# Two-layer cross attention on one core: another order of the calls on all five engines

## The reference

```python
x = L0(x, ctx_768)      # (64, 128, 320), context (64, 128, 192)
x = L1(x, ctx_768)
# L0, 8 heads of 40:
hs  = mha(x @ Wq, enc @ Wk, enc @ Wv)          # enc: the first 124 rows of the context, ca: its last 4
ca_hs1 = mha(ca_q1, x, x)                      # ca_q1 from ca and Wq_ca, keys and values are x itself
ca_hs2 = mha(ca_hs1 @ Wq, ca @ Wk_ca, ca @ Wv_ca)
x = (hs + ca_hs2) @ Wout + b_out + x
# L1, 20 heads of 16:
x = attn(ln1(x), ln1(x), q1, k1, v1) @ o1_w + o1_b + x
x = attn(ln2(x), ctx, q2, k2, v2) @ o2_w + o2_b + x
p = ln3(x) @ ff_w1 + ff_b1; a, g = split(p)    # 2 x 1280 columns
x = (a * gelu(g)) @ ff_w2 + ff_b2 + x
```

## Time and profile before

| what | us |
|---|---|
| three runs, median | 3753.11 |
| lowest, highest | 3748.72, 3754.11 |
| profiled execution | 3752.51 |
| its span, first to last instruction | 3750.7 |
| mean granted clock of TensorE | 0.959 |

### The profile page before, as it was taken

How to read it: one execution, slowest core, us unless ns; L and a number is a source line. 1 busy time by engine, 2 the same in 40 slices (tenths; PEclk the granted TensorE clock), 3 DMA queues, 4 the chain that set the end, 5 groups by cost and what they waited for, 6 DMA issues and landing times.

```text
span 3750.7 us, 114679 instructions
## 1 busy us (share of the span) xinstructions
PE 3433.0 (92%) x38842; PEld 2823.0 (75%) x38842; DVE 2282.8 (61%) x5540; ACT 2431.1 (65%) x4362; POOL 2082.5 (56%) x2307
## 2 busy tenths in 40 slices
PE   7799999999999999999999999999999999999998
PEld 6677777777777777777777777777777777777777
DVE  6566666566666656656665666666566666656664
ACT  3576666667766666776666677666666766666674
POOL 1556555555655555565555556555555655555564
PEclk6899999999999999999999999999999999999999
DMA  5211111221111122211112222111122211112220
GB/s 182 57 42 45 35 44 43 49 53 48 50 34 46 42 49 53 48 51 33 46 41 48 53 49 52 31 47 42 47 53 50 51 31 47 42 46 53 51 50 18
DMA packets 316267, 183.06 MB, mean 49 GB/s; under 512 B 50107, under 2 KB 315379, under 8 KB 315507
## 3 DMA queue, kind: packets, MB, share of 16 engines
q1 hardware_dynamic: 303936, 173.93, 18.4%
q10 hardware_dynamic: 11955, 3.04, 0.4%
HBM read 70.59 MB, written 24.67 MB: 25 GB/s over the span
## 4 chain that ended last, share of the span: by engine, by line
PE 35%; issue 29%; POOL 23%; DVE 8%; DMA 2%; POOLq 1%; ACT 1%; SPq 0%; DVEq 0%; ACTq 0%
PE bank L1487 32%; POOL PT L540 12%; POOL XB L517 2%; DVE mx L1104 2%; POOL cQ L547 2%; POOL cK L547 2%; DMA out<-X 2%; PE bank L1514 1%; POOL XA L517 1%; POOL rstd L598 1%; POOL c L592 1%; DVE OA L1219 1%; DVE hTn L1133 1%; POOL X L517 1%; DVE hTn L1130 1%
## 5 line engine op out<-in xcount | busy, mean ns | idle before, releaser
L540 POOL TENSOR_TENSOR PT<-P,PT 128x512 f16<-128x512 f32 (+1 forms) x924 | 1071.5, 1160 | 603.2 <-ACT PT L811 599.5
L1487 PE MATMUL bank<-hT,w_ff_w 128*128 128x256 f16 x5440 | 637.0, 272 | 0.8 <-DVE hT L1133 0.8
L1104 DVE TENSOR_REDUCE mx<-bank 128x4 f32<-128x512 f32 (+1 forms) x924 | 596.3, 683 | 56.1 <-PE bank L1487 49.4
L1487 PEld LDWEIGHTS bank<-hT,w_ff_w 128*128 128x128 f16 x5440 | 521.4, 98 | 60.7 <-DVE hT L1133 1.2
L1487 PE MATMUL bank<-mxs,pick 84*128 84x128 f16 (+1 forms) x3696 | 553.5, 230 | 0.0
L1487 PE MATMUL bank<-w_ff,F 128*128 128x320 f32 x1360 | 412.2, 438 | 41.6 <-DVE whole L1005 40.4
L1487 PE MATMUL bank<-Qs,Ks 96*128 96x128 f16 x2640 | 404.0, 235 | 15.1 <-DVE mxs L1113 15.1
L1487 PEld LDWEIGHTS bank<-mxs,pick 84*128 84x128 f16 (+1 forms) x3696 | 395.8, 109 | 4.1
L794 ACT ACTIVATE gate<-bank,ff_b,scale 128x256 f32<-128x256 f32 x340 | 187.5, 566 | 304.3 <-PE bank L1487 228.5
L1487 PEld LDWEIGHTS bank<-V,PT 128*128 128x128 f16 (+1 forms) x9504 | 317.0, 96 | 39.5 <-POOL PT L540 13.8
L1487 PE MATMUL bank<-V,PT 128*128 128x17 f16 (+1 forms) x9504 | 341.5, 173 | 0.0
(11 more groups left out here) (289 smaller groups left out, 7386.5 us busy)
## 6 DMA issues: line engine op xcount, KB each, us to landing
Qs<-cQ SPq DMA_DIRECT2D x402, 64.0 KB, 2.6
Ks<-scratch_k SPq DMA_DIRECT2D x99, 160.0 KB, 4.9
Ks<-cK SPq DMA_DIRECT2D x198, 64.0 KB, 2.6
Q0s<-cQ SPq DMA_DIRECT2D x198, 60.0 KB
K0s<-cK SPq DMA_DIRECT2D x198, 60.0 KB
xin<-in_x SPq DMA_DIRECT2D x34, 320.0 KB, 3.6
out<-X SPq DMA_DIRECT2D x64, 160.0 KB, 1.9
xT<-in_xT SPq DMA_DIRECT2D x68, 128.0 KB, 2.1
```

The source lines that it names most:

```text
L540: nc.gpsimd.tensor_tensor(PT[0:keys, n % PT_SLOTS, 1, :], P[0:keys, n % P_SLOTS, :], PT[0:keys, n % PT_SLOTS, 0, :], ALU.subtract).then_in ...
L1104: nc.vector.tensor_reduce(mx[:, g % 2, 4 * u:4 * u + 4], bank[:, :].rearrange("p (h s) -> p h s", h=4)[:, :, 0:keys], axis=AX.X, op=ALU.ma ...
L1487: return nc.tensor.matmul(o, lhsT, rhs, start=start, stop=stop)
```

## The change

`BODY` and the loops of all five engines have the same calls in another order; nothing is added or taken away in the source. The main moves: ff0 and ff1 come to the front of the pass, around Q0T; the S and mx jobs are laid between the chunks; K0T's three chunks go from the first attention to before T4, after outT1_1 and after Q2T; V1_0 and V1_1 go behind S7 and T6; mT and mB, with `extremes_x`, `extremes_context`, `diagonal` and `step_sizes`, go from behind Q2T to the first half of the pass; `next_factors` goes ahead of XT1; K2T2 goes from the end of the pass to before outT2_0; out_proj(0, 1) becomes PE's last call. On SP `load_products` goes behind the nine puts of Q0T, K1T and Q1T, and K0T2 and both stores are later. On ACT gelu 0 and 1 stand apart from 2 and 3, with exps 0 and 1 between, and `load_exp_table` stands before mx0. The diff, indented less:

```diff
@@ -119,12 +119,12 @@
 START = jobs_of("mT mB G")
 BODY = jobs_of("""
-    Q0T0 XT0_0 XT0_1 S0 Q0T1 Q0T2 K1T0 K1T1 K1T2 Q1T0 Q1T1 Q1T2 S1 ff0 S2 S3 ff1 ff2 mx0 K0T0 ff3 T0
-    V1_0 K0T1 mx1 K0T2 V0_0 T1 V1_1 T2 S4 S5 S6 S7 S8 T3 vca mx2 S9 T4 S10 T5 S11 T6 S12 S13 caT0
-    mx3 T7 T8 T9 T10 T11 T12 T13 caT1 ff4 outT1_0 ff5 ff6 ff7 outT1_1 outM1_0 outM1_1 ff8 XT1_0 ff9
-    XT1_1 s4 Q2T0 Q2T1 Q2T2 mT mB V0_1 K2T0 K2T1 y1 S14 S15 S16 S17 S18 mx4 S19 S20 T14 S21 T15 S22
-    S23 T16 S24 S25 mx5 T17 S26 T18 S27 mx6 T19 T20 T21 T22 p4T T23 T24 mx7 outT2_0 T25 y0 T26
-    outM2_0 V2_0 outT2_1 T27 hs0 outM2_1 outT0_0 hs1 XT2_0 V2_1 outT0_1 outM0_0 K2T2 outM0_1 XT2_1 G
+    ff0 Q0T0 Q0T1 XT0_0 Q0T2 XT0_1 ff1 K1T0 K1T1 S0 S1 K1T2 Q1T0 S2 S3 mx0 Q1T1 Q1T2 V0_0 mx1 T0 T1
+    ff2 ff3 S4 S5 T2 vca S6 S7 V1_0 T3 S8 S9 mx2 S10 K0T0 T4 S11 T5 S12 S13 T6 V1_1 mx3 T7 caT0 caT1
+    T8 mT T9 T10 T11 T12 T13 mB ff4 outT1_0 ff5 ff6 ff7 outT1_1 K0T1 outM1_0 outM1_1 ff8 s4 XT1_0
+    XT1_1 ff9 Q2T0 Q2T1 Q2T2 K0T2 S14 S15 y1 S16 S17 S18 V0_1 K2T0 mx4 S19 S20 S21 T14 S22 S23 K2T1
+    S24 T15 S25 mx5 T16 S26 T17 T18 T19 T20 p4T T21 mx6 S27 T22 T23 y0 mx7 T24 T25 K2T2 outT2_0 V2_0
+    outT2_1 T26 T27 outM2_0 hs0 outM2_1 outT0_0 hs1 V2_1 outM0_0 outT0_1 XT2_0 XT2_1 G outM0_1
 """)
 TAIL = jobs_of(" ".join(f"ff{t}" for t in range(FFT)) + " y0 y1")
@@ -447,7 +447,6 @@
     load_step(i + 1)
             def one_pass(i, stores):
-    load_products(i)
     put_low(i, "Q0T", 0, Q0s, cQ, Q_PARTS)
     put_low(i, "Q0T", 1, Q0s, cQ, Q_PARTS)
     put_low(i, "Q0T", 2, Q0s, cQ, Q_PARTS)
@@ -457,18 +456,19 @@
     put_split(i, "Q1T", 0, Qs, cQ, Q_PARTS)
     put_split(i, "Q1T", 1, Qs, cQ, Q_PARTS)
     put_split(i, "Q1T", 2, Qs, cQ, Q_PARTS)
+    load_products(i)
     load_next(i)
     put_low(i, "K0T", 0, K0s, cK, K_PARTS)
     put_low(i, "K0T", 1, K0s, cK, K_PARTS)
     stack_cross_keys(i)
-    put_low(i, "K0T", 2, K0s, cK, K_PARTS)
     put_split(i, "Q2T", 0, Qs, cQ, Q_PARTS)
     put_split(i, "Q2T", 1, Qs, cQ, Q_PARTS)
     put_split(i, "Q2T", 2, Qs, cQ, Q_PARTS)
-    put_out(i, 0, stores)
+    put_low(i, "K0T", 2, K0s, cK, K_PARTS)
     put_next(i, "K2T", 0)
     put_next(i, "K2T", 1)
     put_next(i, "K2T", 2)
+    put_out(i, 0, stores)
     put_out(i, 1, stores)
...
             nc.gpsimd.memset(whole[:, :, :], 0.0).then_inc(split_done, SPLITS_STEP)
             with nc.Fori(0, STEPS + 1, engines=[pool.engine], hint_back_edge=True) as i:
     links[0] = 0
-    last_bias(i)
-    low_context(i)
     low_split(i, "K1T", 0, cK)
     low_split(i, "K1T", 1, cK)
+    low_context(i)
     low_split(i, "K1T", 2, cK)
+    last_bias(i)
     low_split(i, "Q1T", 0, cQ)
     low_split(i, "Q1T", 1, cQ)
+    low_probabilities(i, 0)
     low_split(i, "Q1T", 2, cQ)
-    low_probabilities(i, 0)
     first_bias(i, 0)
+    first_bias(i, 1)
+    zero_bias(i, 0)
+    zero_bias(i, 1)
...
@@ -684,13 +683,14 @@
     low_probabilities(i, 23)
     low_probabilities(i, 24)
     low_probabilities(i, 25)
+    low_x(i)
     low_probabilities(i, 26)
+    low_probabilities(i, 27)
     deviation(i, 2, 0)
-    low_probabilities(i, 27)
-    low_x(i)
     deviation(i, 2, 1)
     deviation(i, 0, 0)
     deviation(i, 0, 1)
+    token_queries(i)
     assert links[0] == POOL_LINKS
             last_bias(STEPS + 1)
...
@@ -880,38 +880,37 @@
     L = LOOP_JOBS
     order.restart()
     links[0] = 0
+    gelu(i, L, 0)
     high_chunk(i, "Q0T", 0, cQ, CH0[0], FQ0)
+    high_chunk(i, "Q0T", 1, cQ, CH0[1], FQ0)
     high_blocks(i, "XT0_0", hTn, 0)
+    high_chunk(i, "Q0T", 2, cQ, CH0[2], FQ0)
     high_blocks(i, "XT0_1", hTn, 1)
-    high_chunk(i, "Q0T", 1, cQ, CH0[1], FQ0)
     split_context(i)
-    high_chunk(i, "Q0T", 2, cQ, CH0[2], FQ0)
+    gelu(i, L, 1)
     high_shifted(i, "K1T", 0, cK, 0)
     high_shifted(i, "K1T", 1, cK, 0)
     high_shifted(i, "K1T", 2, cK, 0)
     high_shifted(i, "Q1T", 0, cQ, 3)
+    load_exp_table()
+    high_maxima(i, 0)
     high_shifted(i, "Q1T", 1, cQ, 3)
     high_shifted(i, "Q1T", 2, cQ, 3)
-    gelu(i, L, 0)
-    gelu(i, L, 1)
+    first_part(i, "V0", 0, V0, HEADS0, D0, fixed[:, F0:F0 + 1])
+    high_maxima(i, 1)
+    exps(i, 0)
+    exps(i, 1)
     gelu(i, L, 2)
-    high_maxima(i, 0)
-    high_chunk(i, "K0T", 0, cK, CH0[0], FK0)
     gelu(i, L, 3)
-    exps(i, 0)
+    exps(i, 2)
     first_part(i, "V1", 0, V1, HEADS1, D1, V1_FACTOR)
-    high_chunk(i, "K0T", 1, cK, CH0[1], FK0)
-    high_maxima(i, 1)
...
+    high_chunk(i, "K0T", 1, cK, CH0[1], FK0)
     gelu(i, L, 8)
+    next_factors(i, L)
     high_blocks(i, "XT1_0", hTn, 0)
+    high_blocks(i, "XT1_1", hTn, 1)
     gelu(i, L, 9)
-    high_blocks(i, "XT1_1", hTn, 1)
     high_shifted(i, "Q2T", 0, cQ, 6)
     high_shifted(i, "Q2T", 1, cQ, 6)
+    split_x(i)
     high_shifted(i, "Q2T", 2, cQ, 6)
     exp4(i)
-    next_factors(i, L)
+    high_chunk(i, "K0T", 2, cK, CH0[2], FK0)
     first_part(i, "V0", 1, V0, HEADS0, D0, fixed[:, F0:F0 + 1])
-    split_x(i)
     high_chunk(i, "K2T", 0, cK, CH1[0], FK2)
-    high_chunk(i, "K2T", 1, cK, CH1[1], FK2)
     high_maxima(i, 4)
...
@@ -1354,52 +1354,53 @@
     L = LOOP_JOBS
     links[0] = 0
     order.restart()
+    ff(i, L, 0)
     low_chunk(i, "Q0T", 0, cQ, CH0[0], FQ0)
+    low_chunk(i, "Q0T", 1, cQ, CH0[1], FQ0)
     low_blocks(i, "XT0_0", hTn, 0)
+    low_chunk(i, "Q0T", 2, cQ, CH0[2], FQ0)
     low_blocks(i, "XT0_1", hTn, 1)
-    maxima(i, 0)
-    low_chunk(i, "Q0T", 1, cQ, CH0[1], FQ0)
-    low_chunk(i, "Q0T", 2, cQ, CH0[2], FQ0)
+    ff(i, L, 1)
     whole_shifted(i, "K1T", 0, 0)
     whole_shifted(i, "K1T", 1, 0)
+    maxima(i, 0)
+    maxima(i, 1)
     whole_shifted(i, "K1T", 2, 0)
     whole_shifted(i, "Q1T", 0, 3)
+    maxima(i, 2)
+    maxima(i, 3)
+    low_maxima(i, 0)
     whole_shifted(i, "Q1T", 1, 3)
     whole_shifted(i, "Q1T", 2, 3)
-    maxima(i, 1)
-    ff(i, L, 0)
-    maxima(i, 2)
-    maxima(i, 3)
-    ff(i, L, 1)
+    low_part(i, "V0", 0, V0, HEADS0, D0, fixed[:, F0:F0 + 1])
+    low_maxima(i, 1)
     ff(i, L, 2)
-    low_maxima(i, 0)
-    low_chunk(i, "K0T", 0, cK, CH0[0], FK0)
     ff(i, L, 3)
-    low_part(i, "V1", 0, V1, HEADS1, D1, V1_FACTOR)
-    low_chunk(i, "K0T", 1, cK, CH0[1], FK0)
-    low_maxima(i, 1)
-    low_chunk(i, "K0T", 2, cK, CH0[2], FK0)
-    low_part(i, "V0", 0, V0, HEADS0, D0, fixed[:, F0:F0 + 1])
-    low_part(i, "V1", 1, V1, HEADS1, D1, V1_FACTOR)
     maxima(i, 4)
     maxima(i, 5)
+    token_values(i)
     maxima(i, 6)
     maxima(i, 7)
+    low_part(i, "V1", 0, V1, HEADS1, D1, V1_FACTOR)
     maxima(i, 8)
-    token_values(i)
+    maxima(i, 9)
     low_maxima(i, 2)
-    maxima(i, 9)
     maxima(i, 10)
+    normalise(i, 0)
+    low_chunk(i, "K0T", 0, cK, CH0[0], FK0)
     maxima(i, 11)
-    normalise(i, 0)
     maxima(i, 12)
     maxima(i, 13)
     normalise(i, 1)
+    extremes_x(i + 1)
+    extremes_context(i + 1)
...
+    norm(i, 2, 0)
     whole_heads(i, 1)
+    norm(i, 2, 1)
+    low_part(i, "V2", 1, V2, HEADS1, D1, fixed[:, F2:F2 + 1])
+    residual(i, 0, 0)
+    low_out(i, 0, 1)
     low_blocks(i, "XT2_0", hT3, 0)
-    low_part(i, "V2", 1, V2, HEADS1, D1, fixed[:, F2:F2 + 1])
-    norm(i, 2, 1)
-    low_out(i, 0, 1)
-    residual(i, 0, 0)
-    low_chunk(i, "K2T", 2, cK, CH1[2], FK2)
+    low_blocks(i, "XT2_1", hT3, 1)
+    low_tokens(i, L)
     residual(i, 0, 1)
     norm(i, 0, 0)
-    low_blocks(i, "XT2_1", hT3, 1)
-    low_tokens(i, L)
     norm(i, 0, 1)
     assert order.next == PER["V"]
     assert links[0] == STEP_LINKS, links[0]
...
@@ -1798,167 +1798,167 @@
             with nc.Fori(0, STEPS + 1, engines=[pe.engine], hint_back_edge=True) as i:
     L = LOOP_JOBS
     filled[0] = 0
+    ff(i, L, 0)
     chunk(i, "Q0T", 0, "Wq", x16, PASSES_X, AT0, CH0)
+    chunk(i, "Q0T", 1, "Wq", x16, PASSES_X, AT0, CH0)
     turn_norm(i, 0, 0)
+    chunk(i, "Q0T", 2, "Wq", x16, PASSES_X, AT0, CH0)
     turn_norm(i, 0, 1)
-    scores(i, 0)
-    chunk(i, "Q0T", 1, "Wq", x16, PASSES_X, AT0, CH0)
-    chunk(i, "Q0T", 2, "Wq", x16, PASSES_X, AT0, CH0)
+    ff(i, L, 1)
     chunk16(i, "K1T", 0, "k1")
     chunk16(i, "K1T", 1, "k1")
+    scores(i, 0)
+    scores(i, 1)
     chunk16(i, "K1T", 2, "k1")
     chunk16(i, "Q1T", 0, "q1")
+    scores(i, 2)
+    scores(i, 3)
+    turn_maxima(i, 0)
     chunk16(i, "Q1T", 1, "q1")
     chunk16(i, "Q1T", 2, "q1")
-    scores(i, 1)
-    ff(i, L, 0)
-    scores(i, 2)
-    scores(i, 3)
-    ff(i, L, 1)
+    values(i, "V0", 0, "Wv")
+    turn_maxima(i, 1)
+    exponents(i, 0)
+    exponents(i, 1)
     ff(i, L, 2)
-    turn_maxima(i, 0)
-    chunk(i, "K0T", 0, "Wk", c16, PASSES_C, AT0, CH0)
     ff(i, L, 3)
-    exponents(i, 0)
-    values1(i, 0)
-    chunk(i, "K0T", 1, "Wk", c16, PASSES_C, AT0, CH0)
-    turn_maxima(i, 1)
-    chunk(i, "K0T", 2, "Wk", c16, PASSES_C, AT0, CH0)
-    values(i, "V0", 0, "Wv")
-    exponents(i, 1)
-    values1(i, 1)
-    exponents(i, 2)
     scores(i, 4)
     scores(i, 5)
+    exponents(i, 2)
+    token_values(i)
     scores(i, 6)
+    scores(i, 7)
+    values1(i, 0)
```

(118 more changed lines are left out.)

90 lines of the change are left out of this document (42 added, 48 removed).

## The result

| | us, median | runs |
|---|---|---|
| before | 3752.45 | 4 |
| after | 3693.81 (3685.34 to 3700.30) | 4 |

The ratio is 0.9844, 95% interval 0.9826 to 0.9863: 1.6% faster, where 3767 us and slower was forecast. The profiled execution took 3700.3 us.

A forecast was written before the change was run, and what follows sets the result against it. PE, 92% busy, was followed as the limit, with ACT or DVE behind it in places. Stages 37.9 + 15.0 + 12.2 + 10.7 + 19.5 + 12.0 + 2.4 = 109.7 us a pass against 109.23, giving 3767 us; range 3660 to 3850.

The forecast's parts named there:

- T7 needs mx3: On PE: T7 must wait for mx3's low part, which stands behind both extremes on DVE; T7 at ff0 + 36.9.
- the new wait of 3.8 us at T7: PE arrives at T7 at 33.1 and waits until 36.9 for the next step's loads, the extremes and mx3.
- clock behind T7: PE behind T7: the gap halves the clock for 6.8 us; cost 1.7 to 3.4 us a pass, taken as 2.4.
- my arrival of PE at T7: PE reaches T7 33.1 us after ff0's start, 11.1 us of work and waits behind S4's start at 22.0.
- 69.4: Pass from T7 to the next ff0, in us: stages of 15.0, 12.2, 10.7, 19.5 and 12.0.
- my 2.7: PE before S4: a new wait of about 2.7 us, arrival at 19.3, Q1T0's last transfer landed at 22.0.
- my 37.9: Stage ff0 to T7: 36.9 to 38.9 us, the middle taken, as half clock at S4 could start the loads later.
- the first issue: SP's first DMA issue for Q0T's chunks: 4.5 us after ff0's start, including a 1.29 us table load.
- The wall of 27 issues on SP: SP issues 27 DMAs for Q0T, K1T and Q1T one after another, 20.3 us in a row, which limits S4.
- The two further table loads: ACT: six table loads a pass for four, both new ones where ACT has time, 0 us beyond the 1.3 counted.
- Rival 3: Slower: the clock halves in both gaps, S4 and T7, every pass; 111.7 us a pass, 3833 us, chance 0.27.
- Rival 1: Faster: gaps of 2.7 and 3.8 us stay, PE's clock holds; 106.3 to 107.3 a pass, 3671 us, chance 0.27.

The follow-up runs named there:

- Experiment 1: Changed kernel with one wait more: on PE, T7 also waits for mx3's low part on DVE; 3878.5 us, ratio 1.0352.
- Experiment 9: Changed kernel with ext_c, diagonal, step sizes, softmax4, mT and mB, with next_factors, split_x and one of the x_values, again behind Q2T2; 3848.1 us, ratio 1.0248.
- experiment 8: Kernel before, with only V0_1 and K2T0 moved to between S18 and mx4, and K2T1 behind S23; 3777.2 us, ratio 1.0062.
- experiment 4: Changed kernel with ff2 and ff3 ahead of T0 and T1 and one load_exp_table left out, four table loads a pass; 3691.0 us, ratio 0.9832.
- experiment 5: Changed kernel with Q0T's chunks split in a free part of F, so SP issues K1T's and Q1T's transfers first; 3616.9 us, ratio 0.9642.
- 12: Changed kernel, no buffer added: Q1T0's transfers ahead of K1T2's on SP, extremes behind caT1, mT behind T11, mB behind ff4; 3634.8 us, ratio 0.9684.
- 7: Kernel of experiment 5 with V1_0, vca, V1_1, T2 and K0T0 ahead of S4, and the extremes, mT and mB later; 3674.9 us, ratio 0.9791.
- experiment 2: Changed kernel with 42 useless matmuls more on PE in the gap before S4; 3687.2 us, ratio 0.9819.
- kernel 10: Kernel of experiment 5 with ff1 moved behind T1 and Q0T2 ahead of K1T0; 3628.3 us, ratio 0.9675.
- 3: Kernel before with 22 useless matmuls more on PE ahead of mx4's transpose; 3719.6 us, ratio 0.9908.

## Why the prediction was wrong

**The step that failed** is "T7 needs mx3". The unit groups are CA 0–1 and 2–3, SELF 4–8 (mx2) and 9–13 (mx3): T7 and T8 belong to the first batch of SELF and need mx2, long done; T9 is the first that needs mx3. PE has caT0, caT1, T8, mT and two products between, and T9 at ff0 + 40.6 waits for nothing. So the new wait of 3.8 us at T7 measured 0, and the term "clock behind T7" (2.4 us a pass, 79 us in all) with it. What the loads' chain did cost PE is the wait at mT, 0.3 us a pass. Experiment 1 put the misread wait into the kernel and got 3878 us.

**A second term was too small, and hid the first.** With the wait at T7 taken out as well as the clock behind it, my sum is 33.1 (my arrival of PE at T7) + 69.4 = 102.5 us a pass, with the clock held at S4; 107.74 was measured. The missing 5.2 us are at S4: a gap 2.0 us longer than my 2.7, and 3.2 us lost to half clock behind it, for which my 37.9 had only the loads' start moved by 1.0. That taking out the 2.4 alone leaves 107.3 us and 3688, close to the 3694 measured, is therefore no proof of the rest of the sum. The terms, forecast and measured in the pass above (108.0 us): ff0 to T7 37.9 and 37.90; to ff7's stretch 15.0 and 14.99; to Q2T2 12.2 and 11.71; to T14 10.7 and 10.59; to outT2_0's low part 19.5 and 20.14; to ff0 12.0 and 12.69.

**That the first term fits is partly luck.** T7 came at + 37.9 not by loads and mx3, but by S4: its gap was 4.71 us where I had 2.7. S4 started at + 23.9 instead of + 22.0, 0.3 of it for the first issue (+ 4.8 for + 4.5) and 1.3 for K1T's nine issues, 7.10 us here and 5.77 before. One of these nine took 1.84 us and the others about 0.6; in the rows of before the long one (1.59) is among Q1T's. What makes an issue long no run shows. PE got there as forecast (+ 19.2 for + 19.3; the working shown gives 19.6). Behind it 6.4 us ran at half clock (1533.15 to 1539.60), 3.2 us lost. 33.1 + 2.0 + 3.2 is 38.3: two errors of 4 to 5 us, one each way, gave 37.9.

**What was right.** Where the old gaps go, and why: the diagonal, the context's extremes, step sizes and softmax4 leave DVE's queue behind Q2T2. Experiment 9 shows that without this there is no gain; experiment 8 that moving V0_1, K2T0 and K2T1 alone brings none. Which of the jobs of experiment 9 counts most is not shown. The wall of 27 issues on SP held in experiment 5. The two further table loads cost nothing that can be told (experiment 4, in which ff2 and ff3 moved too). By an estimate from the drain that the Trainium skill gives (ScalarE: Activation LUTs, What ACT_TABLE_LOAD costs) the first issue would have come 1.4 us later than I forecast, at + 5.9. The trace does not agree: it came at + 4.8. Rival 3's mechanism, two gaps with a half clock behind each, was real but in another kernel: in experiment 9 the gap at S4 and DVE's stand in one pass, and it took 3848 us where rival 3 had 3833; experiment 1, which is rival 3's own case, took 3878.

**The chances.** Rival 1 (3671) came nearest to the time, but said that both gaps stay and the clock holds; one gap stayed and the clock did fall behind it. What I should have weighed is the reading itself: one wait, read from the order of calls and not from the group that T7 belongs to, carried the sign. Without it the sum would have had the right sign and 6.7 us a pass of gain where 1.5 were measured, for the two sizes at S4.

## What to carry to other kernels

Before a wait is put on a path, look up in the code which semaphore value the waiting call asks for and for which units; a batch boundary two units further on is the difference between 3878 us and 3694 here. Take the whole term out of a sum before calling what is left right: the wait stood in the stage's length as well as in the clock. A gap that an engine's queue makes is closed in that queue (experiment 9), or by making its inputs come sooner (5, 12); other work moved into it can open another, since it leaves the place where it was the cover and brings its own waits along (7). Where PE sets the pace, half clock behind a gap of 1 to 2 us cost about 3 us more (2, 10), and a filler that closes one gap can leave the clock to fall at the next. Look at the passes one by one before reading a mean.

## What the runs showed of the hardware

The half clock stood for 6.8 us behind the gap of before in all 31 passes, and for 3.4, 6.8 or 10.2 us behind that of after. By (1 − clock) × 2 × length it was 3.4 us in the first window below (kernel 5), 6.8 in the second (kernel 10) and 10.1 in kernel 8's of 13.00.

```profile
1604.20:1608.20 4.00, 3.80 (x30) 2.85 (x31) 1.52 (x3) 0.54 (x2) 1.15 (x1) 0.57 0.27 74
```

```profile
1724.90:1734.30 9.40, 9.06 (x115) 8.15 (x116) 2.96 (x12) 5.10 (x8) 5.13 (x5) 0.64 0.21 54
```

Which gaps bring it is not settled. 2.52 us did in every pass of before, and 3.5 to 4.95 us in every pass of after; in kernel 10 a gap of 1.51 at mT had it, and one of 1.70 there in the pass before did not; in kernel 8 the same wait at mx4 had it in some passes and not in others, and so had waits of 1.25 and 1.27 us at mT in experiment 2. That makes passes of one program differ by 3 us, within one execution. The same 3.4 us that PE loses cost 1.0 together with the gap where ACT paces (3), 1.9 behind S4 (the changed kernel against the passes of experiment 2 at clock 1.00) and about 3 behind mT (2.9 in kernel 10, 3.3 in experiment 2).
